# A two-layer attention and mixture-of-experts block on one core: stage borders tidied, row maxima placed by a table, router logits as extra projection columns

## The chip, the cores and the metric

One core of one Trainium2 chip runs the whole program. The metric is the device time of one execution in microseconds (us), lower is better. The engines are TensorE (PE), VectorE (DVE), ScalarE (ACT), GpSimd (POOL) and SyncE (SP), which only issues DMAs and waits.

## The reference, cut to what matters

The input x has 4 sequences of 2048 tokens with 256 features; xn is its layer norm. Two branches read xn, and the output is their sum with x.

```python
xn = _layernorm(x)
# branch A: every token for itself, attention BETWEEN its 16 heads of 16 features
Q, K, V = rope(xn@Wq + bq), rope(xn@Wk + bk), xn@Wv + bv
a = softmax(einsum('bsid,bsjd->bsij', Q, K) / 4) @ V
# branch B: causal attention over tokens (16 heads of 16), then a mixture of experts
c   = rmsnorm(xn, g1) @ Wdkv
y   = xn + causal_attention(rmsnorm(xn, g1)@Wq, c@Wuk, c@Wuv) @ Wo
t   = rmsnorm(y, g2)
top_v, top_i = top_k(t @ gate_w, 2);  gates = softmax(top_v)
moe = sum over the 2 chosen of 8 experts:  gate * (silu(t @ w1[e]) @ w2[e])
out = x + a + (y + moe)
```

(The rotation of branch A turns q and k of one token by the same angles and so leaves its scores as they are; the kernel leaves it out.) The causal attention is over 2048 tokens: scores, a maximum per row, the exponential, and products with the values.

## The kernel before, in words

Five stages follow each other, each in a block of its own, at whose end all engines meet.

**Stage 1** (`phase1_project`) goes over 16 chunks of 512 tokens: layer norm, the three projections for branch A (`head_rows`, weights `wh`, one PSUM tile `heads_ps` that DVE empties in `take_heads`), queries and keys of branch B, stored in three bf16 parts, and values (`v_padded`, stored by four DMAs per chunk). From the ninth chunk on PE and DVE also make the row maxima of the first unit. SP loads units 0 and 1 beside that, at its end sets rows of ones in both (`set_ones`, eight DMAs), stores the first maxima, the last heads and values.

**Stage 2** (`phase2_attend`) computes the causal attention in 16 units of 4 heads. A unit has 40 steps: 512 queries against 128 keys each, the last four steps of each of the four query chunks being on the diagonal and narrower. In a step PE makes scores for two halves (`scores`, L1134, two PSUM tiles `st`), ACT their exponentials (`exps`, L1071), and two steps later PE the products with the values (`values`, L1152). The scores already hold minus the row maximum, since q has two extra rows with it (`neg_hi`, `neg_lo`). These maxima of the **next** unit are made beside the current one: 72 pairs, each of which PE scores into two of three PSUM banks (`ring`, `score_pair`, L158), and from which DVE takes two maxima (L1013). `ISSUED` says how many pairs are out after each step; before the change a formula of costs gives it, so that all 72 are out six steps before the unit's end. In a step the order is scores, scores, half of the pairs, values, the rest. At the end of the 72, DVE reduces and splits the maxima (L1020, L1028, L1030), and SP stores four rows of them into q (`store_neg_rows`, L97). PE's first scores of the next unit wait for these rows.

POOL does the branch A attention of two blocks of 128 tokens per unit beside that: it scores them (L921, L926, L929), subtracts the maximum that DVE made at steps 12 and 14 (L935), weighs the values (`weigh_heads`, L942 to L961), and itself issues the store of the result (L964) and the load of the block after next (L910).

SP's queue of stage 2 is written out by hand per unit: at its steps it loads parts of unit n+2 (each waits for PE's progress), stores sums and values (`store_o`, L839), gathers the sums, scatters their inverse (L117), at step 14 stores the quotient of unit n-2 (`store_values`, L130), at step 15, when that has landed, loads eight pieces for the quotient of unit n-1 (`load_values`, L124 and L125), and last stores the maxima's rows:

```python
if n > 1 and i == 14:
    store_values(n - 2)
if n and i == 15:
    load_values(n - 1)
# after the steps
if n + 1 < UNITS:
    store_neg_rows(n + 1, (s + 1) % SLOTS)
```

**Stage 3** (`phase3_route`) goes over 16 chunks: the output projection (L1590), the residual, rms norm (POOL L1389, L1391; DVE L1436), a transpose of the normalised rows (L1600, copied by ACT), the router's logits (L1609), top 2, places by rank, and POOL scatters the rows to their experts by eight indirect DMAs per chunk (L1404). Its start also finishes the quotient of unit 15: sums gathered (L113), reciprocal on DVE (L1417), inverse scattered (L117), loads, POOL's product (L1394), store. **Stage 4** runs the experts, with the other half of branch A beside them, **stage 5** adds up.

## Time and profile before

| | |
|---|---|
| median of 3 runs | 3088.19 us (3088.03 to 3088.95) |
| profiled execution | 3105.57 us |
| its span, first to last instruction | 3104.0 us |
| mean granted TensorE clock | 0.925 |
| busy, share of the span: PE, DVE, ACT, POOL | 82%, 75%, 50%, 73% |
| stage 1 | 0 to about 430 us |
| stage 2 | 430 to 2019 us |
| stage 3 | 2019 to about 2290 us |
| stages 4 and 5 | 2290 to 2907, 2915 to 3104 us |

A share over the whole span mixes five stages with different limits. A busy PE is not PE at its peak, since a matmul's end is modelled. SP has no busy time: what it does is seen in the order and the times of its issues. The granted clock of 1.0 is 2.4 GHz, 0.5 is 1.2 GHz.

### The profile page before, as it was taken

The page shows a single profiled execution, that of the slowest core. Times are in us where ns is not written, and L with a number is a line of the kernel's source. Part 1 is how long each engine was busy: PE and PEld are TensorE (multiplying, and loading weights), DVE is VectorE, ACT ScalarE, POOL GpSimd, SP SyncE. Part 2 cuts the span into 40 slices and gives each one's busy share as a digit, 9 for nine tenths or more (in the row PEclk, how much of TensorE's full clock was granted, in tenths as well). Part 3 has the DMA queues.
Part 4 walks back from the last instruction along what each step waited for, and adds up shares of the span by engine and source line. Part 5 has one row for each costly group of instructions (what it writes and reads, how often), then busy time and mean ns, then how long its engine had stood idle before and what let it go on. Part 6 is the DMA issues. An engine that isn't in the chain of part 4 may idle for free. (4 is left out here: it accounts for less than half of the span.)

```text
span 3104.0 us, 60116 instructions
## 1 busy us (share of the span) xinstructions
PE 2541.4 (82%) x21392; PEld 1305.4 (42%) x21392; DVE 2341.3 (75%) x3764; ACT 1544.4 (50%) x2314; POOL 2252.2 (73%) x1218
## 2 busy tenths in 40 slices
PE   7998968999999999999999999757759888889400
PEld 4544433333333333333333332146647777777400
DVE  4567759888898888988889885035549999999243
ACT  2322236767776767776777777612224444444100
POOL 5443349898989899999989899837736666666476
PEclk9999989999999999999999999967679999999755
DMA  6886542323233232322233211167567666666675
GB/s 191 275 260 210 168 143 56 84 52 83 81 87 76 61 84 78 87 69 70 82 85 86 57 57 42 37 218 244 187 216 213 205 205 204 206 208 211 214 235 187
DMA packets 346973, 435.67 MB, mean 140 GB/s; under 512 B 40858, under 2 KB 276860, under 8 KB 346748
## 3 DMA queue, kind: packets, MB, share of 16 engines
q1 hardware_dynamic: 300796, 350.81, 38.3%
q0 software_dynamic: 17920, 54.55, 5.3%
q10 hardware_dynamic: 28032, 27.27, 2.5%
q8 instruction: 147, 2.41, 0.3%
q14 instruction: 78, 0.64, 0.1%
HBM read 273.43 MB, written 158.47 MB: 139 GB/s over the span
## 5 line engine op out<-in xcount | busy, mean ns | idle before, releaser
L1013 DVE TENSOR_REDUCE p_piece_max<-p_ring 128x1 f32<-128x512 f32 (+3 forms) x2160 | 1281.7, 653 | 186.5 <-PE p_ring L158 97.5
L1071 ACT ACTIVATE p_probs<-p_st 128x1024 f32<-128x1024 f32 (+3 forms) x1280 | 1076.7, 894 | 451.5 <-PE p_st L1134 238.7
L1134 PE MATMUL p_st<-unit_q,unit_k 64*128 64x512 bf16 (+3 forms) x3520 | 417.4, 348 | 27.0 <-SPq L865 17.3
L1152 PE MATMUL p_pv<-p_probs,unit_vg 128*32 128x512 f32 (+3 forms) x3520 | 412.1, 545 | 0.0
L1759 POOL TENSOR_TENSOR p_pv<-p_pr,p_qkv 128x4096 f32<-128x4096 f32 x32 | 347.8, 10868 | 36.3 <-ACT p_pr L1857 35.6
L942 POOL TENSOR_TENSOR p_terms<-p_head_p,p_head_in 128x4096 f32<-128x4096 f32 x32 | 347.8, 10868 | 0.3
L158 PE MATMUL p_ring<-unit_k,unit_q 64*128 64x512 bf16 (+3 forms) x1600 | 272.9, 354 | 69.0 <-DVE p_piece_max L1013 68.6
L1930 PE MATMUL p_y_ps<-p_w,p_hid 128*128 128x256 f32 x1152 | 276.4, 395 | 30.0 <-ACT p_hid L1870 30.0
L921 POOL TENSOR_TENSOR p_terms<-p_head_in 128x4096 f32<-128x4096 f32 x32 | 283.0, 8844 | 7.0 <-POOL p_head_s L929 4.4
L948 POOL TENSOR_TENSOR p_terms<-p_terms 128x2048 f32<-128x2048 f32 (+2 forms) x96 | 252.6, 2631 | 17.1 <-POOL p_terms L948 11.4
L926 POOL TENSOR_TENSOR p_terms<-p_terms 128x2048 f32<-128x2048 f32 (+2 forms) x96 | 252.2, 2627 | 17.2 <-POOL p_terms L926 11.5
L1917 PE MATMUL p_hid_ps<-p_rT,p_w 128*128 128x256 f32 x1152 | 262.1, 381 | 2.2 <-issue 1.8
L1930 PEld LDWEIGHTS p_y_ps<-p_w,p_hid 128*128 128x128 f32 x1152 | 222.2, 198 | 67.0 <-ACT p_hid L1870 37.0
L158 PEld LDWEIGHTS p_ring<-unit_k,unit_q 64*128 64x128 bf16 x1600 | 71.9, 93 | 402.9 <-DVE p_piece_max L1013 388.6
L1917 PEld LDWEIGHTS p_hid_ps<-p_rT,p_w 128*128 128x128 f32 x1152 | 219.5, 191 | 33.5 <-issue 3.4
L1134 PEld LDWEIGHTS p_st<-unit_q,unit_k 64*128 64x128 bf16 x3520 | 142.1, 95 | 207.5 <-ACT p_probs L1071 105.8
L1989 POOL DMA_INDIRECT p_ye<-expert_rows,p_pos x128 | 133.7, 1045 | 79.4 <-issue 78.8
L1152 PE MATMUL p_pv<-p_probs,p_vg 128*32 128x512 f32 (+3 forms) x1600 | 188.0, 547 | 0.0
L1134 PE MATMUL p_st<-p_q,p_k 34*128 34x512 bf16 (+7 forms) x1600 | 187.8, 347 | 0.1
L1404 POOL DMA_INDIRECT sorted_rows<-p_th,p_pos x128 | 130.2, 1017 | 50.4 <-issue 35.7
L1767 POOL DMA_DIRECT2D attn_rows<-p_oh x32 | 18.6, 582 | 198.3 <-DVE p_oh L1820 194.1
L158 PE MATMUL p_ring<-p_k,p_q 64*128 64x512 bf16 (+3 forms) x800 | 135.8, 352 | 32.1 <-DVE p_piece_max L1013 32.0
(188 smaller groups left out, 3678.8 us busy)
## 6 DMA issues: line engine op xcount, KB each, us to landing
p_w<-ffn_w SPq DMA_DIRECT2D x144, 512.0 KB, 5.3
qk_parts<-p_parts SPq DMA_DIRECT2D x64, 384.0 KB, 3.5
head_qkv<-p_heads SPq DMA_DIRECT2D x16, 1536.0 KB, 6.4
p_rows<-sorted_rows SPq DMA_DIRECT2D x72, 256.0 KB, 4.1
expert_rows<-p_y ACTq DMA_DIRECT2D x72, 256.0 KB, 5.6
unit_q<-qk_parts SPq DMA_DIRECT2D x132, 128.0 KB, 3.2
unit_k<-qk_parts SPq DMA_DIRECT2D x132, 128.0 KB, 3.7
p_x<-attn_x SPq DMA_DIRECT2D x32, 512.0 KB, 5.4
```

What stands on the lines that cost most here:

```text
L158: last[half] = nc.tensor.matmul(banks[half][:, k * width:(k + 1) * width], q6[rows, h + k, i * P:(i + 1) * P], k6[rows, h + k, pc * CT:pc ...
L921: step(nc.gpsimd.tensor_tensor(terms[:, :, :, :], head_in[:, u, 0, :, :].unsqueeze(2).to_broadcast([P, H, H, DH]), head_in[:, u, 1, :, :]. ...
L926: step(nc.gpsimd.tensor_tensor(terms[:, :, :, 0:width], terms[:, :, :, 0:width], terms[:, :, :, width:2 * width], ALU.add), before + 2 + k)
L942: step(nc.gpsimd.tensor_tensor(terms[:, :, :, :], head_p[:, u, :, :].unsqueeze(2).to_broadcast([P, H, DH, H]), head_in[:, u, 2, :, :].rear ...
L948: step(nc.gpsimd.tensor_tensor(terms[:, :, :, 0:width], terms[:, :, :, 0:width], terms[:, :, :, width:2 * width], ALU.add), before + 2 + k)
L1013: nc.vector.tensor_reduce(piece_max[:, n % 2, h:h + heads, i, pc], ring_ps[g % RING][:, 0:heads * width].rearrange("p (h k) -> p h k", h=h ...
L1071: nc.scalar.activation(probs[:, 2 * turn_of(s, i) + u, :, 0:width], st_ps[u][:, :, 0:width], ACT.Exp).then_inc(probs_done, 1)
L1134: last = nc.tensor.matmul(st_ps[u][:, half, 0:width], k6[s][rows, PAIR * second + u, kt * P:(kt + 1) * P], q6[s][rows, PAIR * second + u, ...
L1152: last = nc.tensor.matmul(pv_ps[hh * VW:(hh + 1) * VW, skip:CT], vg[s][:, kt, hh * VW:(hh + 1) * VW], probs[:, 2 * turn_of(s, i) + hh % PA ...
L1759: nc.gpsimd.tensor_tensor(pv[:, u, :, :, :], pr[:, u, :, :].unsqueeze(2).to_broadcast([P, H, DH, H]), qkv[:, u, 2, :].rearrange("p (j d) - ...
L1917: last = nc.tensor.matmul(hid_ps[i][:, f * ROW_TILE:(f + 1) * ROW_TILE], w1[:, u, k, (2 * i + f) * P:(2 * i + f + 1) * P], rT[:, k, :], st ...
L1930: last = nc.tensor.matmul(y_ps[t][:, 0:D], hid[:, f, t * P:(t + 1) * P], w2[:, u, f, :], start=f == 0, stop=f == FB - 1)
```

## The change

**Stage 2.** The formula for `ISSUED` becomes a table, and a pair can now also stand between the two scores of a step. Each step has three digits: pairs after the first score, after the second, after the values. One line of the table's 80 steps, and the loop that reads it:

```diff
+    OTHER_UNITS = """
+        100 100 010 101 011 010 011 011 011 111 011 010 011 010 010 111 011 011 011 011
...
                 for i in range(N_STEP):
+                    done = before_step(n, i)
+                    ends = [min(TOTAL, done + sum(spots_of(n)[i][:k + 1])) for k in range(3)]
                     scores(n, s, i, 0)
+                    maxima(done, ends[0])
                     scores(n, s, i, 1)
-                    done, upto = before_step(n, i), ISSUED[n][i]
-                    cut = done + (upto - done + 1) // 2
-                    maxima(done, cut)
+                    maxima(ends[0], ends[1])
                     if i >= LAG:
                         values(n, s, i - LAG)
-                    maxima(cut, upto)
+                    maxima(ends[1], ends[2])
```

In pairs per step, a unit other than the first had 2211222222102232222222102222232222222211 and has 1112212223212113222222221222222222222121. PE at a unit's border, from unit 1 to unit 2, before the change (`p_st` scores, `p_ring` a pair, `p_pv` values, `mask_k` and `mask_q` the diagonal):

```order
L158 MATMUL p_ring<-unit_k,unit_q 128x512 x2
L1152 MATMUL p_pv<-p_probs,unit_vg 32x384 x4
L1152 MATMUL p_pv<-p_probs,unit_vg 32x256 x4
L1152 MATMUL p_pv<-p_probs,unit_vg 32x128 x4
L1134 MATMUL p_st<-p_q,p_k 128x512 x4
L145 MATMUL p_st<-ident_b,mask_k 128x64 x4
L1134 MATMUL p_st<-p_q,p_k 128x512 x4
L145 MATMUL p_st<-ident_b,mask_k 128x64 x4
L158 MATMUL p_ring<-unit_k,unit_q 128x512 x2
```

and with it:

```order
L1212 MATMUL p_pv<-p_probs,unit_vg 32x384 x4
L164 MATMUL p_ring<-unit_k,unit_q 128x512 x2
L1212 MATMUL p_pv<-p_probs,unit_vg 32x256 x4
L1212 MATMUL p_pv<-p_probs,unit_vg 32x128 x4
L1194 MATMUL p_st<-p_q,p_k 128x512 x4
L151 MATMUL p_st<-ident_b,mask_k 128x64 x4
L164 MATMUL p_ring<-unit_k,unit_q 128x512 x2
L1194 MATMUL p_st<-p_q,p_k 128x512 x4
```

The last pair of the unit moved behind the wide values, and the first pair of the next unit in between the two scores.

The loads and stores of branch A move from POOL's queue to SP's, at SP's steps 7 and 14:

```diff
+        HEADS_STORED_AT = (7, 14)
...
+            def load_heads(m, u):
+                wait_apart(sp, head_done, m + 1, apart)
+                sp.dma_start(head_in[:, u, :, :, :].rearrange("p i h d -> p (i h d)"), head_qkv[m]).then_inc(head_loaded[u], 16)
+
+            def store_heads(m, u):
+                wait_apart(sp, head_done, 2 + m + 1, apart)
+                sp.dma_start(attn_rows[m], head_o[:, u, :, :].rearrange("p h d -> p (h d)")).then_inc(head_stored[u], 16)
...
+                    if i in HEADS_STORED_AT:
+                        u = HEADS_STORED_AT.index(i)
+                        store_heads(2 * n + u, u)
+                        if n + 1 < UNITS:
+                            load_heads(2 * n + 2 + u, u)
...
-                wait_apart(pool, head_done, 2 + m + 1, apart)
-                pool.dma_start(attn_rows[bass.ds(m, 1), :, :].rearrange("a p d -> p (a d)"),
-                               head_o[:, u, :, :].rearrange("p h d -> p (h d)")).then_inc(head_stored[u], 16)
```

SP's queue in the second half of a unit from the third on, before the change (`p_vg` a half of the values, `o_with_sums` the store of a query chunk, `o_heads` the quotient):

```order
L83 DMA unit_vg<-v_padded 128x8x128 x2
L839 DMA o_with_sums<-p_pv_sb 17x512 x4
L130 DMA o_heads<-p_raw 128x1024
L124 DMA p_raw<-o_with_sums 32x1024
L125 DMA p_spread<-o_inverse_sums 32x1x1024
L97 DMA unit_q<-p_neg_hi 1x32x128
L97 DMA unit_q<-p_neg_lo 1x32x128
```

and with it:

```order
L88 DMA unit_vg<-v_padded 128x8x128 x2
L896 DMA o_with_sums<-p_pv_sb 17x512 x4
L926 DMA attn_rows<-p_head_o 128x256
L922 DMA p_head_in<-head_qkv 128x768
L136 DMA o_heads<-p_raw 128x1024
L130 DMA p_raw<-o_with_sums 32x1024
L131 DMA p_spread<-o_inverse_sums 32x1x1024
L103 DMA unit_q<-p_neg_hi 1x32x128
L103 DMA unit_q<-p_neg_lo 1x32x128
```

(Repeats of the four `p_raw` and `p_spread` loads and of the four maxima rows stand once.) The two head DMAs came in ahead of the quotient, its loads and the maxima's rows; the first of them waits for POOL's `head_done`.

**Borders.** At stage 2's end SP loads Wo and the first chunk (`first_oT`, `first_xn`, `first_x`, kept in SBUF over the border) and no longer waits for its last stores; these waits stand in stage 3. Stage 3's SP loads chunks 1 and 2 before it gathers the sums; DVE takes the reciprocal after the first two chunks; POOL makes both rms before its product. In stage 1 `set_ones` goes from the end to the start of the second chunk, and the four value stores of a chunk become one with rows of 2 KB. Stages 2 to 4 share one identity matrix.

```diff
+            dve.wait_ge(last_inverse, SUMS_LANDED)
+            nc.vector.reciprocal(inverse[:, :], sums[:, :]).then_inc(last_inverse, 1)
```

(now behind the loop over the first two chunks.)

**Logits.** With y = xn + o·Wo, the logits are rms · (xn·G + o·(Wo·G)), G being gate_w with rows scaled by g2. Stage 1 gets 8 more columns in the third product of `head_rows` and keeps xn·G (`gate_x`, one more DVE operation of 128x8 per block); at its end PE transposes Wo and makes Wo·G (`gate_o`). Stage 3's output projection has 264 columns, DVE adds the 8 logit columns, and the factor rms goes on the difference of the top two alone.

```diff
-                    last = nc.tensor.matmul(heads_ps[:, 2 * D:3 * D], hT[:, s, k, t * P:(t + 1) * P], wh[:, k, 2, :],
+                    last = nc.tensor.matmul(heads_ps[:, 2 * D:3 * D + E], hT[:, s, k, t * P:(t + 1) * P], wh[:, k, 2 * D:],
...
+                nc.vector.tensor_scalar(gate_x[:, bass.ds(n * TT + t, 1), :], heads_ps[:, 3 * D:3 * D + E].unsqueeze(1),
+                                        rms[:, s, t:t + 1], None, ALU.mult).then_inc(heads_taken, 1)
...
             def body(b, c, n, ahead):
-                logits_of(n)
                 if ahead >= 2:
                     project(*after(b, c + 2), n + 2)
-                if ahead >= 1:
-                    transpose_th((c + 1) % NC, n + 1)
                 ranks(n)
```

## Rows read from the trace of the kernel before

**Rows 1.** Windows: start:end, length, busy PE, PEld, DVE, ACT, POOL, clock, DMA, GB/s

```profile
430.20:542.70 112.50, 100.13 (x1125) 36.01 (x1127) 98.17 (x169) 69.53 (x85) 101.39 (x45) 0.94 0.24 60
640.70:1919.60 1278.90, 1190.30 (x13681) 419.41 (x13679) 1122.41 (x1930) 907.25 (x1118) 1154.71 (x508) 0.99 0.28 74
1037.00:1135.00 98.00, 91.28 (x1061) 32.29 (x1057) 87.14 (x150) 69.78 (x86) 87.45 (x39) 1.00 0.28 78
1919.60:2006.00 86.40, 77.09 (x764) 21.33 (x764) 1.25 (x3) 69.25 (x86) 80.04 (x35) 0.94 0.09 28
```

**Rows 2.** Timeline, PE and DVE at a unit's start: start, length, operation, idle before

```profile
1135.05 0.61 PE L1134 MATMUL p_st<-unit_q,unit_k 64*128 64x512 bf16 x4
1136.46 3.77 DVE L1013 TENSOR_REDUCE p_piece_max<-p_ring 128x1 f32<-128x512 f32 x6 [1.45 <-PE p_ring L158]
```

**Rows 3.** Timeline, POOL in the unit from 1037.0: weighing of blocks 0 and 1

```profile
1071.30 10.91 POOL L942 TENSOR_TENSOR p_terms<-p_head_p,p_head_in 128x4096 f32<-128x4096 f32 x1
...
1096.82 0.62 POOL L961 TENSOR_TENSOR p_head_o<-p_head_o,p_head_inv 128x256 f32<-128x256 f32 x1 [0.18 <-POOL p_head_o L960]
...
1099.41 10.84 POOL L942 TENSOR_TENSOR p_terms<-p_head_p,p_head_in 128x4096 f32<-128x4096 f32 x1
...
1124.85 0.62 POOL L961 TENSOR_TENSOR p_head_o<-p_head_o,p_head_inv 128x256 f32<-128x256 f32 x1 [0.18 <-POOL p_head_o L960]
```

**Rows 4.** Timeline, SP's issues at the end of the same unit

```profile
1101.58 0.60 SPq L130 DMA_DIRECT2D o_heads<-p_raw  x1
1111.51 0.31 SPq L124 DMA_DIRECT2D p_raw<-o_with_sums  x1
...
1115.55 0.54 SPq L125 DMA_DIRECT2D p_spread<-o_inverse_sums  x1
1125.46 0.54 SPq L97 DMA_DIRECT2D unit_q<-p_neg_hi  x1
...
1127.31 0.61 SPq L97 DMA_DIRECT2D unit_q<-p_neg_lo  x1
```

**Rows 5.** Timeline, from the start of stage 3 to the first scatter

```profile
2018.90 0.31 POOL L1371 MEMSET p_zeros<- 128x256 f32 x1 [8.48 <-POOLq L752]
...
2030.06 5.33 PE L1590 MATMUL p_mla_ps<-p_wo,p_oT 128*128 128x256 f32 x16 [23.65 <-DMA p_x<-attn_x]
...
2037.42 0.40 ACT L1555 ACTIVATE p_sq<-p_x 128x256 f32<-128x256 f32 x1
...
2036.19 1.52 SPq L117 DMA_DIRECT2D o_inverse_sums<-p_inverse  x1
2044.64 0.34 SPq L124 DMA_DIRECT2D p_raw<-o_with_sums  x1
...
2051.86 2.34 POOL L1394 TENSOR_TENSOR p_raw<-p_raw,p_spread 128x1024 f32<-128x1024 f32 x1 [31.16 <-DMA p_spread<-o_inverse_sums]
...
2074.96 1.33 POOL L1404 DMA_INDIRECT sorted_rows<-p_th,p_pos  x1 [0.18 <-issue]
```

**Rows 6.** Groups by line, 2075 to 2280: busy us, mean ns, idle before

```profile
L1404 POOL DMA_INDIRECT sorted_rows<-p_th,p_pos x128 | 130.2, 1017 | 50.4 <-issue 35.7 <-DVE p_pos L1501 14.6
```

**Rows 7.** Line L130, the quotient's store, 16 times: landing

```profile
DMA to landing us min/median/max: 2.6/9.7/10.1
```

**Rows 8.** Line L97, the maxima's rows, 64 times: landing

```profile
DMA to landing us min/median/max: 1.8/2.6/4.4
```

**Rows 9.** Windows as in rows 1, and PE's timeline in the last unit

```profile
430.20:453.50 23.30, 19.78 (x220) 8.56 (x220) 15.37 (x27) 11.73 (x16) 19.25 (x10) 0.73 0.29 71
1944.00:1961.00 17.00, 11.43 (x84) 2.10 (x80) 0.42 (x1) 10.95 (x14) 16.06 (x8) 0.80 0.03 8
...
1954.19 1.95 PE L1134 MATMUL p_st<-unit_q,unit_k 64*128 64x512 bf16 x8 [4.77 <-ACT p_probs L1071]
```

**Rows 10.** Timeline, SP's issues at stage 1's end

```profile
412.02 5.49 SPq L106 DMA_DIRECT2D unit_k<-ones  x8
...
421.38 4.44 SPq L369 DMA_DIRECT2D v_padded<-p_vx  x4
```

More of the change, by code:

```diff
@@ L189, in phase1_project @@
         ones = keep("ones", [2, CT], BF16)
-        SHARED["until_attended"] = shared
         SHARED["consts"] = (ident, ident_b, mask_q, mask_k, ones)
+        SHARED["chunks"] = (x_v, xn_v, w)
+        gate_o = keep("gate_o", [P, KD, E])
+        gate_x = keep("gate_x", [P, B * NC * TT, E])
+        SHARED["routing"] = (gate_o, gate_x)
         wq = sb("p1_wq", [P, KD, D])
@@ L367, in body @@
                 wait_apart(sp, vx_done, 2 * n + 2, apart)
-                for g in range(NG):
-                    sp.dma_start(v_dram[b, g, c * CT:(c + 1) * CT, :].rearrange("(t p) v -> p t v", p=P),
-                                 vx[:, s, :, g * HG:(g + 1) * HG, :].rearrange("p t h v -> p t (h v)")
-                                 ).then_inc(vx_stored[s], 16)
+                sp.dma_start(v_rows[b, c * CT:(c + 1) * CT, :].rearrange("(t p) x -> p t x", p=P),
+                             vx[:, s, :, :, :].rearrange("p t h v -> p t (h v)")).then_inc(vx_stored[s], 16)
             for b in range(B):
                 for c in range(NC):
+                    if b == 0 and c == 1:
+                        wait_apart(sp, consts, 7, apart)
+                        for _, k6_u, _ in units:
+                            set_ones(sp, k6_u, ones, next_loaded)
                     body(b, c, NC * b + c, b < B - 1 or c < NC - 1)
@@ L708, in _ @@
             chunks(pe, body)
+            pe.wait_ge(maxima_steps, 4)
+            pe.wait_ge(wo_loaded, 16)
+            for j in range(KD):
+                for i in range(KD):
+                    last = nc.tensor.transpose(t_ps[:, j * D + i * P:j * D + (i + 1) * P], x[:, (NC - 1) % 2, i, j * P:(j + 1) * P],
+                                               ident[:, :])
+            last.then_inc(gate_steps, 1)
+            pe.wait_ge(gate_steps, 3)
+            pe.wait_ge(vx_done, 2 * B * NC)
+            for i in range(KD):
+                for j in range(KD):
+                    last = nc.tensor.matmul(cv_ps[:, i * E:(i + 1) * E], rest[:, 0, j * D + i * P:j * D + (i + 1) * P], wh[:, j, 3 * D:],
+                                            start=j == 0, stop=j == KD - 1)
+            last.then_inc(gate_steps, 1)
 def phase2_attend(nc, apart, qk_heads, v_units, o, head_qkv, attn_rows, first_units):
@@ L865, in _ @@
             sp.sem_inc(neg_stored, 64)
+            for u in range(2):
+                load_heads(u, u)
             set_ones(sp, k6[2], ones, ones_set)
@@ L995, in _ @@
             divide(UNITS - 2)
-            for u in range(2):
-                wait_apart(pool, head_stored[u], 16 * UNITS, apart)
         @block.vector
@@ L1185, in phase3_route @@
     sums_of, inverse_of, o = SHARED["sums"], SHARED["inverse"], SHARED["o"]
+    quotients_before, head_stored, o_stored, first_loaded, wo_loaded = SHARED["attended"]
+    first_x, first_xn, first_oT, wo = SHARED["first"]
+    gate_o, gate_x = SHARED["routing"]
     with ExitStack() as ctx:
@@ L1224, in phase3_route @@
         either = sb("p3_either", [P, TT, E], BF16)
+        between = sb("p3_between", [P, TT])
         diff = sb("p3_diff", [P, TT])
@@ L1330, in _ @@
             wait_apart(sp, last_quotient, QUOTIENT_STORED, apart)
+            wait_apart(sp, quotients_before, QUOTIENT_STORED * (UNITS - 1), apart)
+            for u in range(2):
+                wait_apart(sp, head_stored[u], 16 * UNITS, apart)
             def store_res(b, c):
```

243 lines of the change are left out of this document (111 added, 132 removed).

## The prediction

> **What bounds the kernel now.** I read the windows by stage first. Of the span of 3104.0 us, attention (stage 2) takes 1588 us, from 430.2 to the start of routing at 2018.9 [rows 1, 5]. Its 16 units are nearly alike: 112.5 us for unit 0, then 98.0 us, the 13 units 2 to 14 together 1278.9 us (98.4 each) and the last, which has no maxima left to make, 86.4 us [rows 1]. In one unit (1037.0 to 1135.0) PE is busy 91.3 us, DVE 87.1, POOL 87.5, ACT 69.8. PE's busy time holds waiting for the ring of three banks, so DVE, with its 144 reductions, is what sets the pace, and some 11 us of its idle time per unit is what a better table could win. An example: at the unit border DVE idles 1.45 us, since both scores of step 0 go ahead of the first pair [rows 2].
>
> Then I read the queue that nobody counts as an engine, SP. In the same unit POOL starts to weigh head block 0 at 1071.30 (34.3 us after the unit's start), ends block 1 at 1125.47 [rows 3], and by itself issues the DMAs of both. SP meanwhile stores the quotient at 1101.58, waits 9.9 us until it has landed, issues eight loads from 1111.51 to 1116.09, and then waits for DVE's maxima, whose four rows it stores from 1125.46 [rows 4]. They must land before PE may begin the next unit at 1135.05 [rows 2]; the last is issued at 1127.31 and lands 1.8 to 4.4 us later [rows 8], so some 4 us are left over. This slack is what the change touches.
>
> In routing the first scatter starts at 2074.96, 56.1 us after the stage. The chain to it goes through SP's inverse (issued at 2036.19 behind twelve loads, landed at about 2044.6), eight loads, POOL's product at 2051.86 and two rms steps [rows 5]. From there POOL's scatters set the pace; only 14.6 us of 200 are POOL waiting for positions [rows 6].
>
> **The change, part by part.**
>
> *Head DMAs from POOL to SP (the largest term).* POOL loses four DMA issues per unit. Between block 0's end (97.44 in this hundred) and block 1's start (1099.41) lie 1.97 us [rows 3]; without the two issues I leave 0.3, so POOL is done 1.7 us sooner, 52.5 us after it starts weighing instead of 54.2. SP gets them at its steps 7 and 14, and it is in order: the store of block 1 stands **ahead of** the quotient's store, its landing, the eight loads and the four rows of maxima. What could be done by 1116 while POOL was weighing now begins only when POOL has finished. The chain from POOL's end to PE's next unit: 0.15 to wake SP; 0.43 and 0.6 for two issues (like those of rows 4); the quotient's store until landed, 4.2 (its landings lie between 2.6 and 10.1, median 9.7 [rows 7], but the long ones stand right behind value loads and the store of sums, which here are 20 us old, while 512 KB of head data go ahead: nearer the short end); 0.1; the eight loads 4.6 (1111.51 to 1116.09); three issues of maxima before the last, 1.85; the landing of the last, 3.0 (1.8 to 4.4, median 2.6 [rows 8], behind 1 MB of loads). Sum 15.0, bounds 12.3 and 18.
>
> So a unit closes a loop of three pieces: start to weighing, 34.3 now, where I take off 1.4 for the idle border and add 2.0 for TensorE's clock (below): 34.9 (33 to 36.5); weighing 52.5; SP's chain 15.0. That is 102.4 us against 98.4. It holds for units 2 to 14, where the quotient is stored: 13 x 4.0 = **+52 us** (bounds: 98.0, no loss, and 107, +112). In unit 1 the chain lacks the quotient's landing: 97, -1. Unit 0 has neither, and is long enough to hide it.
>
> The clock: after the 17 us that PE stood still at stage 2's start, the granted clock over the first 23.3 us was 0.73, so about half of it ran at 1.2 GHz; in the last unit a wait of 4.77 us was followed by a stretch at half (0.80 over 17 us) [rows 9]. PE will now stand still 5 to 7 us per unit; I take the shorter case, 2 us, because the steps after the border are narrow and hold few pairs.
>
> Here the Trainium skill (Trainium Kernel Development and Optimization, Key Constraints) speaks for another outcome: DMAs of SP, ACT and POOL run on the same 16 DMA engines, and issuing from several of them saves only the sequencer's issue time. By that rule the move is worth POOL's 1.7 us and costs SP some 1.2 us of issue, so that the loop would stay open. It leaves out the wait that the issue carries along; which is right, the next unit's start shows. It is rival 1.
>
> *Maxima by a table.* The 72 pairs and the place by which they are complete (step 33) stay; only the spread over the steps changes, and a pair may now stand between the two scores. DVE's work stays 87.1 us. Where SP's chain closes the loop, a faster unit only waits longer. It pays in unit 0 alone, where DVE is busy 98.2 of 112.5 [rows 1]: I take -4 (0 to -8).
>
> *Stage 2's end.* The last unit gets its heads earlier (POOL is ahead, the 4.77 us wait [rows 9] goes), but its quotient chain, 0.6 + 3.5 + 4.6 + 3 and POOL's product 2.4, now follows POOL's last block. Weighing from 29, +52.5, +14.1, +2 to the next stage: 97.7 against 99.3 (1919.6 to 2018.9): -2 (-5 to +8).
>
> *Routing's start.* Chunk 0 and Wo are in SBUF already, so PE begins 2 us after the stage instead of 11 [rows 5]. DVE now does both first chunks before the reciprocal: PE and ACT of chunk 0 as now (2030.06 to 2037.8), rms and scaling 3.4, then 7 for chunk 1: about 21 us. Then SP's inverse, quiet, 3.2; eight loads and their landing 7.3; product 2.4; rms step 1.6: first scatter at 36 instead of 56, **-20** (-12 to -24). *Its loop*: transposes, their copies and logits go from PE and ACT, and DVE reads logits that are two chunks old. POOL keeps eight scatters of 1.02 us with 0.30 between them and 1.6 for the rms steps, 12.1 us per chunk, and at most the 14.6 us of waits [rows 6] go: **-9** (0 to -14). The half clock of PE there hides behind POOL.
>
> *Stage 1.* The eight DMAs of ones (5.5 us of SP) and three of four value stores (3.3) leave SP's last stretch [rows 10] before PE starts stage 2 at 430.2 [rows 1], but 2.5 MB of heads and values still have to land: -5. Wo's load, transposes and products on PE fit beneath that landing. Against it stands one 128x8 product on DVE per block, with the heads' bank released 0.1 us later, in 64 blocks, most of them off the path, and 8 more columns: +2. Together -3 (-8 to +5). Experts and combine: 0.
>
> **Sum**: +52 - 4 - 1 - 2 - 20 - 9 - 3 = **+13 us** on the profiled execution of 3105.6. The three timed runs have a median of 3088.2, 17.4 below the profiled one; the same difference gives **3101 us**. About 0.2%, 6 us, is what a measurement of this kernel can tell from no change.
>
> **The rivals.**
>
> *1. SP's chain stays hidden.* The place is the start of units 3 to 15: if the four rows land before PE is ready, which is so if the chain after POOL takes under some 8 us, units run as DVE lets them. With a third of its idle time won, 95 us each: 14 x 3.4 = -48 in place of +51; 3002 us. For it speaks the rule above, and the quotient's landing of 2.6 [rows 7]; against it that the eight loads, the three issues and one landing alone take over 8 us in these rows. 0.12.
>
> *2. The chain closes the loop, but cheaply.* Landing and maxima at their short ends and no loss to the clock: 99.4 per unit, +13 instead of +52: 3062 us, faster than before. It decides between the signs from 101.4 us per unit downward. 0.2.
>
> *3. PE stays at 1.2 GHz* after each stall as long as at the stage's start (half of 23 us): 4 us more per unit, 3153 us. 0.13.
>
> *4. Routing's start does not shrink:* the loads of chunks 1 and 2, 3 MB, go ahead of the sums and the inverse; then DVE waits for them and the first scatter comes as late as now: +20, 3121 us. 0.1. The logits by extra columns would then do no more than what they say, and nothing for the time.
>
> **How the numbers follow.** My forecast has 0.45. The range leaves out rival 1 and the far end of rival 3: 3058 to 3145. Faster: rival 1, most of rival 2 and the short end of the forecast, 0.31; within 0.2%: 0.15; slower: 0.54.
>
> **What would show it.** Right: PE waits at the first scores of units 3 to 15 for SP, 5 to 7 us, with units of 101 to 104 us; SP issues the quotient's store within 2 us of POOL's last product and the maxima's rows 10 us later, while DVE had split them long before; the first scatter 34 to 38 us into routing, 12.1 us per chunk. Wrong: units below 98 us with no wait of PE for SP (then the chain is mispriced or hidden), or a unit longer than 105 us at a clock below 0.9. If units 0 and 1 alone gain more than 8 us, the table was worth more than I gave it.

## The result, and the profile after

The changed kernel takes **3134.9 us** (median of 4 runs, 3130.6 to 3139.4) against 3088.1 for the kernel before on the same chip: a ratio of 1.0155, 95% interval 1.0135 to 1.0174, or **+47 us**. The forecast was slower, by 13 us, in a range that holds the measured time. The side, the place and the mechanism of the loss were right. The sum was 34 us short: four smaller terms (the table in unit 0, stage 1, routing's start and routing's loop), each of which was to give time back, gave less than forecast or cost some.

The later runs came in four batches, each on a chip of its own. The kernel before took 3103.8 and 3109.1 us on the first two, 3090.0 and 3089.7 on the last two. The profile under the prediction is of the slower sort (3105.6), the timed runs beside it and the changed kernel's first profile of the quicker. I speak of slower and quicker chips; as each was used once, a chip and the hour of its runs are not told apart. To take stages apart I use pairs of profiles from one chip, of batch 2 (slower) and batch 4 (quicker), where the changed kernel stood at 1.0130 (1.0103 to 1.0158) and 1.0137 (1.0112 to 1.0162). The borders are the first scores of a unit, POOL's first instruction of stage 3, scatters, and the load of stage 4's table.

| stretch, us | forecast | quicker chip | slower chip |
|---|---|---|---|
| stage 1 | -3 | 427.1 to 429.9: +2.8 | 428.4 to 433.5: +5.1 |
| unit 0 | -4 | 112.6 to 115.2: +2.6 | 112.6 to 116.1: +3.5 |
| unit 1 | -1 | 98.0 to 96.4: -1.6 | 98.0 to 96.6: -1.4 |
| units 2 to 14 | **+52** | 1277.3 to 1329.2: **+51.9** | 1276.1 to 1330.4: **+54.3** |
| unit 15, to stage 3 | -2 | 99.5 to 96.2: -3.3 | 99.6 to 96.6: -3.0 |
| to the first scatter | -20 | 56.4 to 41.9: -14.5 | 55.9 to 41.2: -14.7 |
| from there to the last chunk's | -9 | 182.0 to 182.0: 0 | 195.0 to 189.3: -5.7 |
| last chunk's scatters | 0 | 9.0 to 8.8: -0.2 | 9.1 to 8.9: -0.2 |
| last scatter to stage 4's table | 0 | 6.1 to 5.4: -0.7 | 5.4 to 13.1: +7.7 |
| stages 4 and 5 | 0 | 815.9 to 818.9: +3.0 | 822.3 to 824.6: +2.3 |
| span | +13 | 3083.7 to 3124.0: +40 | 3102.4 to 3150.3: +48 |

The windows of the changed kernel's profile (units 0, 2 to 14, the seventh, and the last), in the columns of [rows 1]:

```profile
434.50:550.40 115.90, 100.69 (x1125) 34.97 (x1125) 97.91 (x169) 70.35 (x85) 105.12 (x43) 0.95 0.26 58
647.30:1976.30 1329.00, 1221.96 (x13675) 423.74 (x13675) 1134.63 (x1930) 907.45 (x1119) 1127.30 (x457) 0.96 0.31 72
1056.10:1157.70 101.60, 93.68 (x1059) 32.57 (x1061) 88.12 (x150) 69.82 (x86) 85.52 (x36) 0.97 0.33 75
1976.30:2056.40 80.10, 76.13 (x744) 21.54 (x744) 1.26 (x3) 68.06 (x84) 70.65 (x31) 0.95 0.03 10
```

DVE's instructions are as many as in [rows 1]; what a unit has gained in length is waiting. The page of the changed kernel names it: PE's first scores now wait for the rows of maxima, 41.3 + 16.3 us of the 1329, or 4.4 us per unit:

```profile
L1194 PE MATMUL p_st<-unit_q,unit_k 64*128 64x512 bf16 (+3 forms) x3520 | 446.5, 357 | 68.9 <-DMA unit_q<-p_neg_lo 41.3
...
L1194 PE MATMUL p_st<-p_q,p_k 34*128 34x512 bf16 (+7 forms) x1600 | 201.4, 357 | 22.6 <-DMA p_q<-p_neg_lo 16.3
```

The timeline at that unit's end shows SP's chain, which answers to [rows 3, 4]: POOL's last product of block 1, SP's issues, PE's first scores.

```profile
1142.46 0.62 POOL L1030 TENSOR_TENSOR p_head_o<-p_head_o,p_head_inv 128x256 f32<-128x256 f32 x1 [0.18 <-POOL p_head_o L1029]
...
1143.18 0.37 SPq L926 DMA_DIRECT2D attn_rows<-p_head_o  x1
1143.66 0.36 SPq L922 DMA_DIRECT2D p_head_in<-head_qkv  x1
1144.13 0.39 SPq L136 DMA_DIRECT2D o_heads<-p_raw  x1
1148.83 0.32 SPq L130 DMA_DIRECT2D p_raw<-o_with_sums  x1
...
1153.04 0.54 SPq L131 DMA_DIRECT2D p_spread<-o_inverse_sums  x1
1153.70 0.54 SPq L103 DMA_DIRECT2D unit_q<-p_neg_hi  x1
...
1155.80 0.58 SPq L103 DMA_DIRECT2D unit_q<-p_neg_lo  x1
...
1157.68 1.04 PE L1194 MATMUL p_st<-unit_q,unit_k 64*128 64x512 bf16 x4 [4.26 <-DMA unit_q<-p_neg_lo]
```

From POOL's end (1143.08) to PE's start are 14.6 us; the forecast had 15.0. The quotient's store (L136) is issued 1.05 us behind POOL's end, and its landing holds SP for 4.7 us; in [rows 4] it went out while POOL was at work.

In stage 3 (from 2072.60), beside [rows 5]: DVE's first sum, its reciprocal, SP's load of g2 and its inverse, POOL's product and the first scatter.

```profile
2086.95 0.17 DVE L1481 TENSOR_TENSOR p_logits<-p_mla_ps,gate_x 128x16 f32<-128x16 f32 x1 [12.73 <-DMA p_g<-ffn_g]
...
2100.92 0.54 DVE L1507 RECIPROCAL p_inverse<-p_sums 128x64 f32<-128x64 f32 x1
...
2077.41 2.93 SPq L1372 DMA_DIRECT2D p_g<-ffn_g  x1
...
2101.56 0.34 SPq L123 DMA_DIRECT2D o_inverse_sums<-p_inverse  x1
...
2111.05 2.34 POOL L1450 TENSOR_TENSOR p_raw<-p_raw,p_spread 128x1024 f32<-128x1024 f32 x1 [11.75 <-DMA p_spread<-o_inverse_sums]
...
2115.06 1.24 POOL L1458 DMA_INDIRECT sorted_rows<-p_th,p_pos  x1 [0.20 <-issue]
```

PE had chunk 0 ready by 2082.2, but DVE stands 12.7 us for the gains, whose load SP issues as its fourth: a wait that the forecast did not have.

### The profile page after: what moved, and what is told of

The parts are those of the page before. It is cut to its first block and busy times, and to the rows that moved or that the text cites. A ratio compares the mean times of both kernels' runs of the same rounds, so it can differ in the third digit from the quotient of the medians.

```text
span 3130.1 us, 59306 instructions
## 1 busy us (share of the span) xinstructions
PE 2529.8 (81%) x21020; PEld 1258.3 (40%) x21020; DVE 2361.9 (75%) x3865; ACT 1529.2 (49%) x2282; POOL 2212.8 (71%) x1150
## 3 DMA queue, kind: packets, MB, share of 16 engines
q1 hardware_dynamic: 285212, 367.85, 41.3%
## 5 line engine op out<-in xcount | busy, mean ns | idle before, releaser
L1194 PE MATMUL p_st<-unit_q,unit_k 64*128 64x512 bf16 (+3 forms) x3520 | 446.5, 357 | 68.9 <-DMA unit_q<-p_neg_lo 41.3
L1017 POOL TENSOR_TENSOR p_terms<-p_terms 128x2048 f32<-128x2048 f32 (+2 forms) x96 | 252.2, 2627 | 17.1 <-POOL p_terms L1017 11.4
L995 POOL TENSOR_TENSOR p_terms<-p_terms 128x2048 f32<-128x2048 f32 (+2 forms) x96 | 251.5, 2620 | 17.1 <-POOL p_terms L995 11.4
L1944 PEld LDWEIGHTS p_y_ps<-p_w,p_hid 128*128 128x128 f32 x1152 | 222.4, 198 | 68.9 <-ACT p_hid L1886 38.9
L1194 PE MATMUL p_st<-p_q,p_k 34*128 34x512 bf16 (+7 forms) x1600 | 201.4, 357 | 22.6 <-DMA p_q<-p_neg_lo 16.3
L1811 DVE TENSOR_TENSOR p_prod<-p_q_ps,p_qkv 128x4096 f32<-128x4096 f32 x32 | 141.5, 4421 | 33.2 <-ACT p_q_ps L1866 33.2
L1458 POOL DMA_INDIRECT sorted_rows<-p_th,p_pos x128 | 131.6, 1028 | 37.5 <-issue 35.4
```

What stands on the lines that cost most here:

```text
L1017: step(nc.gpsimd.tensor_tensor(terms[:, :, :, 0:width], terms[:, :, :, 0:width], terms[:, :, :, width:2 * width], ALU.add), before + 2 + k)
L1194: last = nc.tensor.matmul(st_ps[u][:, half, 0:width], k6[s][rows, PAIR * second + u, kt * P:(kt + 1) * P], q6[s][rows, PAIR * second + u, ...
L1944: last = nc.tensor.matmul(y_ps[t][:, 0:D], hid[:, f, t * P:(t + 1) * P], w2[:, u, f, :], start=f == 0, stop=f == FB - 1)
```

## The experiments

**Batch 1 (kernel before: 3103.8 us). Is it SP's chain?** Four kernels, of which three edit the changed kernel and one the kernel before.

```diff
-        HEADS_STORED_AT = (7, 14)
+        HEADS_STORED_AT = (7,)
...
                    store_neg_rows(n + 1, (s + 1) % SLOTS)
+                store_heads(2 * n + 1, 1)
+                if n + 1 < UNITS:
+                    load_heads(2 * n + 3, 1)
```

> The changed kernel, with the store and the load of head block 1 issued by SP behind the rows of maxima instead of at its step 14. Theory A (the loss in stage 2 is SP's chain: it cannot store the quotient, load the values and store the maxima before POOL has ended block 1): the chain opens. SP stores the quotient some 45 us into a unit and the maxima right after DVE's split, PE no longer waits for them, and units 2 to 14 take what DVE's reductions allow, 94 to 97 us instead of 102.2: 13 x (102.2 - 95.5) = 87 us less, 3048 us. Rival B (the time lies in the units themselves: the table of pairs, or the heads' DMAs going by another queue): units stay above 101 us and the time stays above 3115 us.

Measured: 3057.1 us, 0.9850 of the kernel before (0.9834 to 0.9867). Every unit from 1 to 13 takes 96.2 us, and PE's wait for the maxima's rows is gone. SP in the unit from 1024.9, and POOL's end of block 1:

```profile
1102.17 0.37 SPq L136 DMA_DIRECT2D o_heads<-p_raw  x1
1110.51 0.31 SPq L130 DMA_DIRECT2D p_raw<-o_with_sums  x1
...
1115.44 0.54 SPq L103 DMA_DIRECT2D unit_q<-p_neg_hi  x1
...
1117.29 0.59 SPq L103 DMA_DIRECT2D unit_q<-p_neg_lo  x1
1118.31 0.88 SPq L926 DMA_DIRECT2D attn_rows<-p_head_o  x1
...
1110.17 0.62 POOL L1033 TENSOR_TENSOR p_head_o<-p_head_o,p_head_inv 128x256 f32<-128x256 f32 x1 [0.18 <-POOL p_head_o L1032]
```

Theory A holds, with one number off: the quotient goes out 77 us into the unit, not 45. Two waits of SP stand ahead of it. The stores of chunk 2's output wait for its values, and keep the quotient to 64.6 us in the next kernel too, as in [rows 4]. The other 12 us come with head block 0's store at step 7: until POOL has ended block 0, 60 us into the unit, SP stands at that store, with loads of unit n+2 and output stores behind it. The quotient is under way while POOL still weighs, and in units 2 to 13 the rows land 0.9 to 2.7 us before PE needs them (3.5 to 5.5 in the next kernel): block 0's store costs slack here, and no time.

The second kernel takes `store_heads` and `load_heads` out of SP and puts the two DMAs back behind POOL's last product:

```diff
+                wait_apart(pool, head_done, 2 + m + 1, apart)
+                pool.dma_start(attn_rows[bass.ds(m, 1), :, :]...).then_inc(head_stored[u], 16)
...
+                    load_heads(2 * n + 2 + u, u)
```

> The changed kernel with all DMAs of the head blocks issued by POOL again, as before the change; the rest of the change stays. Theory A: units 2 to 14 fall to 94 to 97 us, POOL's two blocks take 54.1 us again instead of 52.1, and SP's quotient stands 45 us into the unit; 3050 us, within 6 us of the kernel with block 1's DMAs behind the maxima. Rival B (not the queue but the table is at fault): above 3110 us. Should this one be over 10 us slower than the other, POOL's 2 us per unit are on the path.

Measured: 3063.1 us, 0.9867 (0.9851 to 0.9884); units of 96.4 to 96.8, POOL's blocks 54.2 us again. Rival B fails: the table does not lengthen units. The kernel is 6 us slower than the first one, under the 10 us that would have put POOL's 2 us per unit on the path.

The third is the kernel before with only `store_heads` and `load_heads` in SP's steps 7 and 14.

> The kernel before with this one part of the change alone: the DMAs of the head blocks go from POOL to SP, at steps 7 and 14. Theory A: units 2 to 14 lengthen from 98.4 to about 102.3 us, and the time by 51 us, to 3139 us. Rival B (the table of pairs is what lengthens the units): at most 3098 us.

Measured: 3181.1 us, **1.0251** (1.0214 to 1.0289), +77 us. Units 2 to 14 take 1361.8 us, 104.8 each. That is more than theory A's 51 us: the part costs more alone than with the table. Windows of the first 23 us of two of its units; the granted clock (third number from the right) is 0.72:

```profile
1157.00:1180.00 23.00, 20.79 (x200) 7.67 (x202) 15.66 (x26) 13.55 (x17) 21.21 (x9) 0.72 0.17 40
1262.80:1285.80 23.00, 20.79 (x200) 7.66 (x202) 15.65 (x26) 13.54 (x17) 21.21 (x9) 0.72 0.18 41
```

The same in two units of the changed kernel (101.2 and 103.9 us long):

```profile
1157.70:1180.70 23.00, 21.47 (x256) 8.66 (x260) 17.91 (x30) 16.82 (x21) 21.21 (x9) 0.90 0.23 54
1258.90:1281.90 23.00, 22.15 (x230) 8.40 (x230) 16.36 (x27) 15.51 (x20) 21.21 (x9) 0.80 0.21 50
```

and in one of the kernel with block 1 last, where PE does not stand at the border:

```profile
1121.10:1144.10 23.00, 21.17 (x274) 8.30 (x272) 19.84 (x34) 17.54 (x22) 21.83 (x7) 1.00 0.27 67
```

POOL starts to weigh 33.8 us into a unit at clock 1.00, 35.2 at 0.90 and 36.8 at 0.80; with the old order 34.3 at 1.00 and 38.9 at 0.72. A later start is a later end of POOL, and so comes back through the loop.

The fourth is the changed kernel with the old `ISSUED` and PE's old loop (both scores, then the pairs).

> The changed kernel with the pairs of the maxima spread over the steps as before (by the planner's costs, both scores of a step ahead of them). Theory A: as SP's chain closes the unit, the table buys nothing there: units 2 to 14 stay at 102 us and the time within 8 us of the changed kernel's 3135. Unit 0, which took 115.9 us instead of 112.4, tells whether the table cost it: back at 112.5 if so. Rival B (the table is at fault): over 30 us faster.

Measured: 3168.7 us, 1.0212 (1.0194 to 1.0230), 18 to 25 us slower than the changed kernel at its ratios of 1.0155 or 1.0130. Theory A is wrong on the units: 2 to 14 take 1351.9 us, 22 more, so the table does buy something in a closed loop. It is right on unit 0, which is back at 111.8.

**Batch 2 (3109.1 us).** Both kernels again:

> The kernel before once more, to have the profiled executions of both kernels from one chip. In the first pair of profiles the two differ by 26.5 us, in the timed runs by 46.8. Theory A (the 17 us by which the profiled execution of the kernel before stood above its timed median belong to that execution and its chip, not to profiling, so they may not be carried over to another kernel): here the spans of the two profiles differ as the times do, by 40 to 55 us, and the profiled span lies within 8 us of this label's own median. Rival B (profiling adds 17 us to whatever kernel): the profiled span stands 12 to 22 us above this label's median.

> The changed kernel on the same chip, the other half of the pair. Theory A: 44 to 50 us slower than the kernel before, and stage by stage: stage 1 +2 to +4, unit 0 +4, unit 1 -1 to -2, units 2 to 14 +50 to +56 together, the way to routing's first scatter -14, routing's loop -9, stages 4 and 5 within 3 us. Rival B: stages 4 and 5 are faster by the 9 us that the first pair of profiles showed, and the units' loss is smaller than 50.

Measured: 3108.1 and 3150.7 us, spans 3102.4 and 3150.3: 47.9 apart. Theory A holds: each profile's span lies within 6 us of the median of its own runs, and profiling adds no 17 us. The table above has the stretches.

```diff
-                    if i in HEADS_STORED_AT:
+                    if i == HEADS_STORED_AT[0]:
...
                        load_values(n - 1)
+                    if i == 15:
+                        move_heads(n, 1)
```

> The changed kernel with SP's steps in another order: the store of the quotient and the loads of the values go ahead of head block 1's store and load, which stay ahead of the rows of maxima. So of SP's chain behind POOL's last block only two head issues, the rows' four and one landing are left: 0.15 + 1.2 + 1.85 + 3.5 = 6.7 us. POOL's end in an open unit stands at 85.9, so the rows land at 92.6, before PE's 96.2. Theory A (the quotient's landing and the eight loads behind POOL's last block are what closes the loop): the same as with block 1 wholly behind the maxima, units of 96.2 to 97 us, 75 to 82 us less than the changed kernel. Rival B (any wait of SP for POOL ahead of the rows closes it, as the 1 MB of value loads and the head's load slow the rows' landing): units of 99 or more.

Measured: 3065.1 us, 0.9860 (0.9833 to 0.9886), 86 us less than the changed kernel. Ten of thirteen units take 96.2 or less, the others 97.0 to 98.0. SP in the unit from 1028.6:

```profile
1105.35 0.37 SPq L136 DMA_DIRECT2D o_heads<-p_raw  x1
1113.69 0.31 SPq L130 DMA_DIRECT2D p_raw<-o_with_sums  x1
...
1118.39 0.52 SPq L926 DMA_DIRECT2D attn_rows<-p_head_o  x1
1119.04 0.35 SPq L922 DMA_DIRECT2D p_head_in<-head_qkv  x1
1119.52 0.55 SPq L103 DMA_DIRECT2D unit_q<-p_neg_hi  x1
...
1121.63 0.58 SPq L103 DMA_DIRECT2D unit_q<-p_neg_lo  x1
```

So it is what stands **behind** the waiting store, the quotient's landing and the eight loads, that closes the loop, not the wait for POOL. The rows land at 95 to 98, not at my 92.6: the loads end 4 us behind POOL, since the quotient took 8.3 us to land here. In the three units of 97.0 to 98.0 us the rows come just too late and PE stands 0.7 to 1.7 us.

The next kernel has block 1 last, unit 0's pairs as the planner had them, and in stage 3 the order g2, sums, chunks 1 and 2, with the reciprocal ahead of chunk 1.

> The kernel with block 1's DMAs behind the maxima, and two more edits, each to be read in its own stage. (1) Unit 0's pairs spread as by the planner before: if the table's first row of steps is at fault there (DVE reaches the head blocks' maxima at 31.7 us, 9 us before POOL has scored block 1), unit 0 falls from 115.9 to 112 us; the rival (SP's heads' loads are at fault) leaves it at 116. (2) Stage 3: g2's load first, then the sums, then chunks 1 and 2; the reciprocal between the two first chunks. If DVE's wait of 12.7 us for g2 behind three slower loads is what keeps the first scatter at 41 us instead of my 36, it comes 28 to 34 us after the stage's start; the rival (chunk 1's loads then come late and DVE waits for them instead) 38 or more. Time: 12 to 16 us less than the kernel with block 1 behind the maxima alone.

Measured: 3053.2 us, 0.9816 (0.9792 to 0.9840); by the two ratios 10.6 us less than with block 1 last alone, for the forecast's 12 to 16. Unit 0 falls to 111.4: the table's first line was at fault. DVE's maxima of head block 1 and PE's next scores in the changed kernel's unit 0,

```profile
475.36 0.42 DVE L1100 TENSOR_REDUCE p_head_max<-p_head_s 128x16 f32<-128x256 f32 x1 [4.91 <-POOL p_head_s L998]
...
477.64 1.03 PE L1194 MATMUL p_st<-unit_q,unit_k 64*128 64x512 bf16 x4 [5.91 <-ACT p_probs L1131]
```

and DVE in this kernel, without a wait (the unit starts at 434.5 there and at 429.5 here):

```profile
470.25 0.41 DVE L1103 TENSOR_REDUCE p_head_max<-p_head_s 128x16 f32<-128x256 f32 x1
```

The first scatter came at 39.9 us, so here the rival won: SP stood 8 us for the last sums, with chunk 1's loads behind that wait.

**Batch 3 (3090.0 us).**

```diff
             sp.dma_start(g2[:, :], ...)
+            load(0, 1)
+            load(0, 2)
             for slot in range(2):
                 wait_apart(sp, o_stored[slot], ...)
             gather_sums(...)
-            load(0, 1)
-            load(0, 2)
```

> The kernel with the mended starts, stage 3 once more: g2's load first, then chunks 1 and 2, and only then the wait for the last sums and their load (with the sums second, SP stood 8 us before chunk 1's loads, and PE and DVE waited for chunk 1 until 22 us into the stage). The reciprocal stays between the two chunks. Theory A: chunk 1 is there when DVE has done chunk 0, the last rms step that POOL takes ahead of the first scatter comes some 7 us earlier, and the first scatter at 31 to 35 us instead of 39.9; time 5 to 8 us less than with the sums second (3047 on that chip). Rival B (the sums' way through DRAM, then the inverse's, decides alone): 38 or more.

Measured: **3032.5 us, 0.9821 (0.9805 to 0.9838)**, 57 us under the kernel before and, by the ratios, some 100 under the changed one. What the new order of loads is worth in time can't be read from this: the kernel ahead of it had 0.9816 on a slower chip, where the new stage 3 gains more (see routing's loop below). The first scatter comes at 36.7, between the theories. DVE and POOL in stage 3 (from 1978.9):

```profile
1997.42 0.55 DVE L1509 RECIPROCAL p_inverse<-p_sums 128x64 f32<-128x64 f32 x1 [7.97 <-DMA p_sums<-o_with_sums]
...
2006.82 2.34 POOL L1453 TENSOR_TENSOR p_raw<-p_raw,p_spread 128x1024 f32<-128x1024 f32 x1 [2.32 <-DMA p_spread<-o_inverse_sums]
2013.99 0.19 POOL L1446 TENSOR_SCALAR p_rrms<-p_ss 128x4 f32<-128x4 f32 x1 [4.83 <-ACT p_sq L1615]
...
2015.62 1.24 POOL L1461 DMA_INDIRECT sorted_rows<-p_th,p_pos  x1 [0.24 <-issue]
```

DVE now stands for the sums, and POOL, after its product, 4.8 us for chunk 2's squares: its third rms step goes ahead of the first scatter.

> The same kernel, with the 2 MB store of zeros issued by SP ahead of routing's loop instead of behind it. Behind it, it fills the DMA queues for 8 us; in that time DVE stands 8 us before the last chunk's places, and SP then takes 0.7 us for each register instruction of its first two stores of zeros, so that the way from the last scatter to stage 4 is 17 us instead of the 5.5 of the kernel before. Theory A (DVE and SP wait for their next instructions behind the 2 MB): the wait of DVE goes, SP's eight stores take 9 to 10 us and end under POOL's scatters, stage 4 starts 5 to 7 us behind the last scatter, and the time falls by 8 to 11 us. Rival B (the slow stretch comes from something else, for instance from the jump out of the loop): last scatter to stage 4 stays at 15 us or more, time within 3 us, or slower, where the 2 MB now delay the loads of chunks 4 and 5.

Measured: 3034.5 us, 0.9827 (0.9811 to 0.9844). Neither wait was there in the kernel beside it on this chip, so nothing is decided. From the second chunk's scatters to the third's are 16.3 us for 12.5: this is what the 2 MB delay.

```diff
+                if t < TT - 1:
+                    nc.vector.tensor_scalar(gate_x[:, B * NC * TT - TT + t + 1:..., :], heads_ps[:, 3 * D:3 * D + E]...)
                 nc.vector.tensor_scalar(gate_x[:, bass.ds(n * TT + t, 1), :], ...)
```

> The same kernel as the one with the loads first, with one cost of stage 1 doubled: in 48 of the 64 blocks DVE takes the logits' product a second time (into a place that is overwritten later; the result is the same). Stage 1's last chunk starts 5 to 7 us later since the change: 0.2 us per chunk without pairs and 0.5 per chunk with them. Theory A (DVE's product, with the bank of the heads released later, is what costs it): another 0.15 us per early and 0.35 to 0.4 per late chunk, stage 1's last chunk 3.5 to 5 us later than in the kernel beside it. Rival B (the 8 more columns on PE): less than 1.5 us.

Measured: 3037.2 us, 0.9835 (0.9815 to 0.9854). Chunks without pairs take 20.8 us for 20.7; of those with pairs, two that nothing else disturbed take 28.4 for 28.1 and 29.8 for 29.6. That makes 2.1 to 2.8 us over stage 1, less than theory A's 3.5 and more than rival B's 1.5. Its last chunk starts 7.4 us later, but 2.4 of that lie ahead of the first chunk and 1.9 each in two single chunks, as they differ between runs of one kernel too.

The fourth is the kernel of batch 1 with the heads' DMAs on SP, block 1's now behind the maxima.

> The kernel before with the heads' DMAs on SP, those of block 1 behind the rows of maxima: the move without the chain. POOL gains 2 us per unit, but ends 9.5 us before the unit's end anyway. Theory A (the queue that issues the DMAs is worth nothing by itself; the unit is set by DVE's reductions and their spread): units stay at 98.0 us and the time within 5 us of the kernel before, 70 us under the run with block 1's DMAs at step 14. So the gain of the changed kernel with block 1 last is the table's 1.8 us per unit and routing's. Rival B (POOL's 2 us are on the path): units of 96.2 to 97, 14 to 25 us faster.

Measured: 3082.5 us, 0.9976 (0.9966 to 0.9985), 7.4 us faster. Units 2 to 14 take 1280.1 us, as before. In the profiles (beside batch 4's of the kernel before) the gain lies in the last unit, 90.7 us to stage 3 for 99.5. That unit makes no maxima, and POOL, which has saved 2 us per unit, is 5.2 us ahead in it (weighing from 28.6 for 33.8). Block 0's store still stands at step 7 here, so that it is block 1's place that costs the 77 us. The rule of the Trainium skill (Trainium Kernel Development and Optimization, Key Constraints) that issuing from several engines saves only issue time describes this kernel, whose units stay as they were, and not the one with the store at step 14: the ratios of the two to the kernel before are 1.0251 and 0.9976, 85 us apart, with the same DMAs on the same queue.

**Batch 4 (3089.7 us)**, for the two terms still open.

> The kernel before, profiled for this batch. The chips differ: runs of this kernel took 3088 to 3090 us on one and 3104 to 3109 on another. Theory A: where it takes 3090 us, the 17 us less lie at places where an engine's sequencer stands without a wait that the trace names (DVE's 8 to 16 us before the last chunk's places, routing's loop, the two units of 99.6 us), and its units are otherwise the same 98.0; where it takes 3106, the spans repeat those of the second batch within 4 us per stage. Rival B: everything is longer by 0.5% alike.

> The changed kernel beside it. By the second batch: stage 1 +5, unit 0 +3.5, unit 1 -1.5, units 2 to 14 +50 to +55, the last unit -3, routing's first scatter -14 to -15, its loop -6 to -9. From the last scatter to the load of stage 4's table: on a chip with 3090 us for the kernel before 5.4 us in both; on one with 3106, 12 to 13 us against 5.4.

Measured: 3090.0 and 3131.8 us. The kernel before is quicker than in batch 2 in two places: routing's loop, 182.0 for 195.0, and the stages behind it, 815.9 for 822.3; units are the same. The waits of DVE in routing (us, times, longest), kernel before on the slower chip,

```profile
DVE p_place L1491 <- remote: 54.1, 15, 8.1
```

and on the quicker, where that line is absent:

```profile
DVE p_th L1436 <- POOL p_rrms L1391: 43.8, 14, 3.7
```

Of 1103 register instructions of SP, 63 take over 0.55 us (most 0.7) on the slower chip and none on the quicker; in the prediction's profile they are 46. They all lie behind the first scatters, between 2078 and 3070 us. Every profile of batches 1 and 2 has 54 to 68 of them, and none of batches 3 and 4 has one.

> The changed kernel with one edit: the 2 MB store of zeros goes ahead of routing's loop. Theory A (what makes DVE and SP stand at routing's end is the 2 MB in front of their next instructions): on a 3106 us chip DVE's wait of 8 us before the last chunk's places is gone, and so are SP's register instructions of 0.7 us; the table's load comes 5 to 6 us after the last scatter instead of 13, and the time falls by 3 to 8 us (a longer gap of some 4 us at the second or third chunk takes part of it). Rival B: on such a chip both waits stay. On a 3090 us chip, where the waits are absent, both say 0 to +5 us, and nothing is decided.

Measured: 3136.3 us, 1.0152 (1.0135 to 1.0169). The chip is a quicker one, and again nothing is decided.

```diff
                                                ALU.mult, ALU.add)
-                nc.vector.tensor_scalar(gate_x[:, bass.ds(n * TT + t, 1), :], ...)
```

> The changed kernel without DVE's product for the logits in stage 1 (gate_x is zero; the x part of the router's logits is left out), the 8 columns on PE kept. Doubling the product in three of four blocks cost 0.1 us per chunk without pairs and 0.25 with them. Theory A: DVE's product is two thirds of stage 1's loss: chunks of 20.55 us and 28.2 to 28.3 instead of 20.7 and 28.6, the last chunk 3 to 4 us earlier. Rival B: it is all of it, 20.45 and 28.1, as in the kernel before. Rival C: under a third, 20.65 and 28.5.

Measured: 3121.3 us, 1.0103 (1.0082 to 1.0123). Chunks take 20.6 and 28.2 to 28.3 us, in the kernel before 20.5 and 28.1 to 28.2, in the changed one 20.7 and 28.6 to 28.7. DVE's product is half of the early chunks' loss and four fifths of the late ones': 7 x 0.1 + 7 x 0.4 = 3.5 us. The 8 columns are left with 7 x 0.1 + 7 x 0.1 = 1.4. This is theory A: from the first chunk's start to the last chunk's the kernel takes 3.0 us less than the changed one, for the forecast's 3 to 4.

## Why the forecast was right, and where it failed

**Head DMAs: right in mechanism and size.** Units 2 to 14 grew by 51.9 to 54.3 us for +52. The pieces hold within 0.5 us: weighing from 35.4 (forecast 34.9), weighing 52.1 (52.5), the chain 14.7 (15.0); that the sum agrees better than its pieces is luck. That the order of SP's steps does it, and what stands behind the store, is shown by three kernels that differ in nothing else: with the store at step 14 102.3 us per unit, behind the values 96.4, behind the maxima 96.1. Rivals 1 and 2 fell with it. Rival 3 had the right effect at a smaller price: weighing starts 1.3 to 3.2 us later than at full clock, 1.6 in the mean, for my 2.0. PE's wait at the border was 3.5 to 5.3 us, not the 5 to 7 that I named as a sign.

**The table: what I said of it was wrong twice.** "Where SP's chain closes the loop, a faster unit only waits longer. It pays in unit 0 alone." The four kernels of one size say:

| us per unit, 2 to 14 | old order | table |
|---|---|---|
| SP's chain open | 98.2 | 96.1 |
| chain closed | 104.0 to 104.8 | 102.3 |

The table is worth 2.1 us in an open unit. In a closed one it is worth 1.7 to 2.5, as POOL starts to weigh at 35.4 us for 37.2 to 37.8 with the old order; some of this was in my piece of 34.9. And in unit 0, where I took -4, it costs 2.6 to 3.5: DVE comes to the maxima of step 14 4.9 us before POOL has scored block 1, and DVE, ACT and PE wait in turn.

**Stage 1, forecast -3, measured +2.8 to +5.1.** Its end did shrink, by 3.1 (35.3 to 32.2 us from PE's first product of the last chunk into `heads_ps` to stage 2; I had -5). The step that failed is "most of them off the path ... +2": 64 DVE products and 8 columns cost 4.9 us over the undisturbed chunks, all of it on the path. The rest of a pair's difference is scatter: single chunks are 1 to 2 us longer in one run than in another, and stage 1 took 426.1 to 430.3 us in five profiles with the old stage 1 and 428.0 to 434.5 in eleven with the new one (without the two that change its work), 3.4 apart in the mean.

**Routing's start, forecast -20, measured -14.5.** The failed step is "DVE now does both first chunks before the reciprocal: ... about 21 us": it was 28, most of it because g2's load is fourth on SP's queue. So the first scatter came at 41.2 to 42.5 us, outside the 34 to 38 that I gave as a sign. With g2 first the wait is gone, and two others show, for the sums and for chunk 2's squares; 36.7 is what was reached.

**Routing's loop, forecast -9, measured 0 and -5.7.** This is the largest miss on a quicker chip, and the step that failed is "at most the 14.6 us of waits [rows 6] go": the 14.6 us that POOL waited for positions belong to the slower chips. There the term was about right: in batch 1 the loop took 195.9 us with the old stage 3 and 183.5 to 184.8 in the three kernels with the new one, and POOL's waits for positions 18.1 and 2.5 to 2.7. On a quicker one the same group of the kernel before and of the changed one reads (110 and 120 scatters in the window):

```profile
L1404 POOL DMA_INDIRECT sorted_rows<-p_th,p_pos x110 | 117.9, 1071 | 32.0 <-issue 31.1 <-ACT p_sq L1555 0.6 <-DVE p_pos L1501 0.3
```

```profile
L1458 POOL DMA_INDIRECT sorted_rows<-p_th,p_pos x120 | 123.9, 1032 | 35.1 <-issue 32.7 <-ACT p_sq L1611 2.1 <-DVE p_pos L1557 0.3
```

POOL is held by its own scatters there, 0.3 us of 182 go on positions, and what leaves PE, ACT or DVE has nothing to win. I took a wait from a profile 17 us above the timed runs and did not ask what in it those 17 us were.

**Routing's end on the slower chips, forecast 0, measured +7.7**, and nothing on the quicker ones. SP's eight stores of zeros, kernel before and changed kernel in batch 2:

```profile
2265.93 10.02 SPq L1357 DMA_DIRECT2D sorted_rows<-p_zeros  x8
```

```profile
2306.23 16.77 SPq L1414 DMA_DIRECT2D sorted_rows<-p_zeros  x8
```

Before, they end with POOL's last scatter; after, they start 2.3 us later behind DVE's last places (2301.3 and 2263.3), take 6.8 longer, and end 9 us behind the last scatter. Batch 1 repeats it: 6.1 us from the last scatter to the table with the old stage 3, 11.4 to 13.3 with the new. Why SP's instructions take 0.7 us there stays open: both runs that moved the 2 MB store fell on chips without it.

**The last unit, -2, measured -3**: right. Stages 4 and 5 took 2 to 3 us more, which no run explains. The misses add up to 27 us on the quicker chip (stage 1 5.8, unit 0 6.6, routing's start 5.5, its loop 9, the last stages 3, less 3 of small gains) and to 35 on the slower. The 34 us of the timed runs lie in between the two pairs, whose intervals both hold the ratio of 1.0155.

## What to carry to other kernels

When a DMA moves to an in-order queue, price the wait that it brings by what stands behind it in the program: here the same DMAs cost 77 us with block 1's at step 14 and gain 7 with them behind the maxima. Put a DMA that waits for a busy engine behind everything that the next stage needs. And before an idle time is counted as gain, see whether it is there in a profile whose time is that of the timed runs.

## What was not expected of the hardware

Two sorts of chip show in one kernel's times (3090 and 3104 to 3109 us). The slower do not differ in the units (98.0 us in both) or in the granted clock of stages 1 and 2 (0.98 and 0.99 in both), but in single engines' sequencers from routing on. There register instructions of SP take 0.7 us, 46 to 68 of them, and DVE has waits in routing that the profile puts down to "remote", 54.1 us in batch 2's kernel before; the quicker chips show neither. The cause is not known.

PE's granted clock over a unit's first 23 us was 1.00 where PE had not stood at the border. Otherwise it did not go by the length of that wait: 0.90 after 4.26 us and 0.80 after 3.54 in the changed kernel, 0.72 after 2.90 with the old order of pairs.

The quotient's store of 512 KB took 4.2 to 4.8 us to land when issued behind POOL's last block. With block 1's DMAs moved behind it, at 77 us into the unit and right behind four output stores, it took 8.2 to 8.3; in the kernel before, at 64.5 us and also right behind four output stores, mostly 9.8 to 10.1.
